# Graph layer with routed experts on one core: one normalized tensor for the router and the experts, and expert outputs weighted in place and added in DRAM

## The reference, cut to what matters

```python
xn = layernorm(x)
x = x + gnn(xn, W, edges) + linear_attention(xn, wq, wk, wv, wo)
#   gnn: h = xn @ W; deg = 1 + in-degree without self edges; dinv = 1/sqrt(deg)
#        out[src] = sum over edges and loops of dinv[src] * dinv[dst] * h[dst]
xt = layernorm(x)                                   # normalized once
logits = xt @ Wr + br                               # 8 experts
top_p, top_idx = top_k(softmax(logits), 2); weights = top_p / top_p.sum()
xn2 = layernorm(xt)                                 # normalized twice
xe = xn2[None] * ln_g[:, None] + ln_b[:, None]      # per expert
h = gelu(xe @ W1 + b1)
y = h @ W2 + b2
out = x + (weights[:, :, None] * y[top_idx]).sum(axis=1)
```

## Time and profile before

| | us |
|---|---|
| median of 3 runs | 2603.84 |
| the profiled execution, device time | 2604.59 |
| its span, first to last instruction | 2602.70 |
| edge sums, 450 to 1589.5 | 1139.5 |
| routing, 1589.5 to 1680 | 90.5 |
| picks up to the first expert product, 1680 to 1771.2 | 91.2 |
| experts, 1771.2 to 2536.9 | 765.7 |
| output, 2536.9 to 2602.7 | 65.8 |

### The profile page before, as it was taken

How to read it: one execution, slowest core, us unless ns; L and a number is a source line. 1 busy time by engine, 2 the same in 40 slices (tenths; PEclk the granted TensorE clock), 3 DMA queues, 4 the chain that set the end, 5 groups by cost and what they waited for, 6 DMA issues and landing times.

```text
span 2602.7 us, 56074 instructions
## 1 busy us (share of the span) xinstructions
PE 2180.6 (84%) x12041; PEld 1796.9 (69%) x12042; DVE 1328.7 (51%) x2437; ACT 1200.7 (46%) x3274; POOL 1324.0 (51%) x1388
## 2 busy tenths in 40 slices
PE   0999994888888888888888866658999999999990
PEld 0677773666666666666666645517999999999980
DVE  8799996565666666666666546651111111111116
ACT  2444441666666666666666644502333333333320
POOL 6766565677777777777777761002222222222220
PEclk9999997899999999999999997558999999999995
DMA  4000003333333333333333494434555555555539
GB/s 135 1 1 1 1 1 112 93 105 105 104 104 105 105 105 105 105 105 105 105 104 104 122 80 69 132 124 137 180 180 180 181 179 182 181 180 181 181 108 297
DMA packets 139535, 304.96 MB, mean 117 GB/s; under 512 B 29056, under 2 KB 77101, under 8 KB 139376
## 3 DMA queue, kind: packets, MB, share of 16 engines
q0 software_dynamic: 59232, 143.39, 21.9%
q1 hardware_dynamic: 80272, 161.23, 17.4%
HBM read 270.55 MB, written 33.98 MB: 117 GB/s over the span
## 4 chain that ended last, share of the span: by engine, by line
PE 57%; DMA 20%; DVE 9%; issue 5%; DVEq 4%; POOL 3%; ACT 0%; SPq 0%; ACTq 0%; POOLq 0%
PE B L1403 18%; DMA BIG<-table,W2A 18%; PE B L1499 15%; PE B L1508 14%; DVEq L665 3%; DVE BIG L660 3%; PE B L1392 2%; PE B L1465 1%; POOL BIG L507 1%; PE B L1309 1%; PE B L1342 1%; DVE W1A L1061 1%; POOL W2A L483 1%; PE B L1487 1%; PE B L1326 1%
## 5 line engine op out<-in xcount | busy, mean ns | idle before, releaser
L507 POOL DMA_INDIRECT BIG<-table,W2A x880 | 834.5, 948 | 301.3 <-issue 202.4
L547 DVE TENSOR_TENSOR ACC<-ACC,B 128x512 f32 x880 | 605.4, 688 | 451.9 <-PE B L1403 312.3
L1403 PE MATMUL B<-BIG 128*128 128x256 f32 x1760 | 429.8, 388 | 83.9 <-DMA BIG<-table,W2A 81.7
L1403 PE MATMUL B<-BIG,W2A 128*128 128x256 f32 x1760 | 427.6, 386 | 85.9 <-DMA BIG<-table,W2A 85.8
L1079 ACT ACTIVATE BIG<-B,SMALL 128x128 f32<-128x128 f32 (+1 forms) x889 | 251.1, 387 | 506.3 <-PE B L1499 506.3
L1403 PEld LDWEIGHTS B<-BIG 128*128 128x128 f32 x1760 | 322.4, 191 | 182.9 <-issue 143.6
L1403 PEld LDWEIGHTS B<-BIG,W2A 128*128 128x128 f32 x1760 | 316.8, 190 | 174.3 <-issue 137.2
L1499 PEld LDWEIGHTS B<-BIG,W1A 128*128 128x128 f32 x3360 | 393.6, 193 | 7.9 <-DVE BIG L550 2.6
L1499 PE MATMUL B<-BIG,W1A 128*128 128x128 f32 x3360 | 394.4, 276 | 2.0 <-DVE BIG L550 2.0
L1508 PE MATMUL B<-W2A,BIG 128*128 x1680 | 380.1, 379 | 0.7 <-DVE ACC L547 0.7
L1508 PEld LDWEIGHTS B<-W2A,BIG 128*128 128x128 f32 x1680 | 311.0, 190 | 39.1 <-issue 1.1
(11 more groups left out here) (208 smaller groups left out, 2203.8 us busy)
## 6 DMA issues: line engine op xcount, KB each, us to landing
W1A<-in_w SPq DMA_DIRECT2D x105, 1024.0 KB, 5.1
BIG<-table,W2A POOLq DMA_INDIRECT x880, 2.8
W2A<-in_w SPq DMA_DIRECT2D x1, 8192.0 KB, 30.1
table<-ACC SPq DMA_DIRECT2D x7, 896.0 KB, 7.1
token_x<-BIG SPq DMA_DIRECT2D x49, 128.0 KB, 1.7
W2A<-in_x SPq DMA_DIRECT2D x1, 6144.0 KB
W1A<-pick_y SPq DMA_DIRECT2D x4, 896.0 KB, 10.8
W2A<-pick_y SPq DMA_DIRECT2D x4, 896.0 KB, 11.2
```

Of the source, the lines that this page charges most:

```text
L507: pool.indirect_dma_start(G[h][:, u, :], None, table, bass.IndirectOffsetOnAxis(ap=idx_s[h][:, u:u + 1], axis=0)).then_inc(gath[h][u // 2] ...
L547: return dve.tensor_tensor(o, a, b, op)
L1403: last = mm(B[u][:, k * D:(k + 1) * D], OH[h % 2][:, u, k * P:(k + 1) * P], G[h][:, u, :], start=True, stop=True)
```

## The change

In the edge sums, `acc` now takes the input and the attention too, each multiplied by `sdeg` = sqrt(deg), so that `acc * dinv` is the new x without a separate `residual` pass: `add_attention` writes to `acc`, and a new `add_inputs` does one VectorE instruction for each of 49 tiles.

In routing, one normalized tensor remains, `xs2`. Its scales come from the statistics of `acc` (with `dinv` worked in), it is both stored to `token_x` and transposed for the router, in pairs of tiles, and the logits are multiplied by `unscale` afterwards, which turns the twice normalized rows back into once normalized ones for the router. Groups are 6, 10, 16 and 17 tiles. All copies of transposes are ScalarE's, 512 columns at a time. Behind them ScalarE multiplies `acc` by `dinv` in place (49 instructions), and then signals `res_ready`.

In the picks, `pc_tile` and `pc_tokens` get a second buffer, and ScalarE makes the second half of `pc_tokens`.

In the experts, the two gates of every node are transposed on TensorE, stored to a table `gates` in DRAM, and gathered by slot (`gather_gate`, 128 numbers for each tile). `sums` in DRAM starts as a copy of `acc` (6.5 MB, one SP transfer). `outputs` adds `b2` into `y_plain`, which frees the bank, and multiplies by the gate into `y_out`; the scatter adds its rows to `sums` in DRAM instead of writing `pick_y`, and each scatter waits until the one before has landed, since the two picks of a node may be in neighbouring tiles. ScalarE's index copies are gone.

The output is one DRAM to DRAM transfer from `sums` to `out`.

```diff
 sync:
-            with sp.Fori(0, NT // RG) as g:
-                store_group(g)
-            sp.wait_ge(x_done, 1)
+            for j in range(NPAIR):
+                n = min(2, NT - 2 * j)
+                sp.wait_ge(xs_ready, 2 * j + n)
+                sp.dma_start(token_x[2 * j * P:(2 * j + n) * P, :]..., xs2[j % 4][:, 0:n, :]).then_inc(xs_out[j % 4], 16)
             sp.dma_start(W2A[:, :]..., w2...).then_inc(w2_in, 16)
...
             for t in range(4):
                 load_w1(t, t)
+            sp.wait_ge(gates_T_ready, 1)
+            sp.dma_start(gates[0:PICKS * P, :]..., gates_T...).then_inc(gates_out, 16)
+            sp.wait_ge(res_ready, 1)
+            sp.dma_start(sums.rearrange("(t p) d -> p t d", p=P), acc).then_inc(sums_set, 16)
             with sp.Fori(1, ST // 4) as i:
...
-            (loads of pick_y in 9 parts, stores of out in 9 parts)
+            sp.dma_start(out.rearrange("(p a) d -> p (a d)", p=125), sums[0:N_NODES, :].rearrange("(p a) d -> p (a d)", p=125)
+                         ).then_inc(o_sent, 16)
 gpsimd:
+            def scatter_y(t):
+                pool.wait_ge(y_ready, t + 1)
+                if t >= 1:
+                    pool.wait_ge(y_sent[(t - 1) % 2], 16 * ((t + 1) // 2))
+                pool.indirect_dma_start(sums, bass.IndirectOffsetOnAxis(ap=slot_row[:, t:t + 1], axis=0),
+                                        y_out[t % 2], None, compute_op=ALU.add).then_inc(y_sent[t % 2], 16)
...
+            pool.wait_ge(sums_set, 16)
+            for t in range(ST):
+                scatter_y(t)
+                if t + 3 < ST:
+                    gather_gate(t + 3)
+                if t + 5 < ST:
+                    gather_x(t + 5)
 vector:
+            ch.add(dve.tensor_copy(sdeg, col[12][:, 0:NT]))
+            ch.add(tt(dinv2, dinv, dinv, ALU.mult))
...
             def add_attention(t):
+                dve.drain()
-                tt(xt, xt, B[7][:, 0:D], ALU.add).then_inc(q_added, 1)
+                dve.scalar_tensor_tensor(out=a, in0=B[7][:, 0:D], scalar=sdeg[:, bass.ds(t, 1)], in1=a,
+                                         op0=ALU.mult, op1=ALU.add).then_inc(q_added, 1)
+            def add_inputs(t):
+                dve.drain()
+                dve.scalar_tensor_tensor(out=a, in0=xt, scalar=sdeg[:, bass.ds(t, 1)], in1=a, op0=ALU.mult, op1=ALU.add)
...
             def slot_digits(g, s):
+                when(dve, tk_v, pc_used, g - 1)
                 tt(pc_at[s], pc_digits, cols(slot_at, P), ALU.is_equal)
-                tt(pc_tile, ...); dve.drain(); when(dve, tk_v, pc_used, g)
-                tt(pc_tokens[:, 0:ST, :], ...); ts(pc_tokens[:, ST:2 * ST, :], pc_tile, row_1, ALU.mult)
+                tt(pc_tile[s], ...); dve.drain(); dve.sem_inc(pc_ready, 1)
+                tt(pc_tokens[s][:, 0:ST, :], ...); dve.drain(); dve.sem_inc(pc_ready, 1)
...
             def outputs(t, s):
-                when(dve, tk_v, y_sent[s], (t - s) * 8)
-                tt(y_out[s], B[7][:, 0:D], b2_all[:, bass.ds(e * D, D)], ALU.add).then_inc(y_ready, 1)
+                tt(y_plain, B[7][:, 0:D], b2_all[:, bass.ds(e * D, D)], ALU.add).then_inc(y_free, 1)
+                dve.drain()
+                when(dve, tk_v, gate_in[s], (t - s) * 4 + 16)
+                when(dve, tk_v, y_sent[s % 2], (t - s % 2) * 8)
+                ts(y_out[s % 2], y_plain, slot_gate[:, bass.ds(t, 1)], ALU.mult).then_inc(y_ready, 1)
+                dve.drain()
 scalar:
+                    cp(xs2[j % 4][:, t % 2, :], acc[:, t, :], ACT.Identity, scale=rstd2[:, t:t + 1], bias=nmr2[:, t:t + 1]
+                       ).then_inc(xs_ready, 1)
+                    if t % 2 == 1 and t >= 3:
+                        transposed_x2(t // 2 - 1)
...
+            for t in range(NT):
+                last = cp(acc[:, t, :], acc[:, t, :], scale=dinv[:, t:t + 1])
+            last.then_inc(res_ready, 1)
...
+                cp(pc_tokens[g % 2][:, ST:2 * ST, :], pc_tile[g % 2], scale=row_1).then_inc(pc_rows, 1)
 tensor:
-                when(pe, tk_t, y_ready, t)
+                when(pe, tk_t, y_free, t)
```

More of the change, by code:

```diff
@@ L66 @@
 SLOTS = ST * P
[L67 to L70, removed]
+LGROUPS = [range(a, b) for a, b in zip((0, 6, 16, 32), (6, 16, 32, NT))]
+NPAIR = (NT + 1) // 2
 PICKS = TOPK * NT
@@ L79 @@
 assert NGR <= 32 and UNROLL * 5 < 24
-assert NT % RG == 0 and STEPS >= NT + 2 + 2 * E // BATCHES and min(RLAG) >= 3
+assert all(g.stop % 2 == 0 for g in LGROUPS[:-1])
 assert PICKS % PC == 0 and PC % 2 == 0 and (PICKS // PC) % 2 == 1 and ST % 4 == 1
@@ L178, in gps_layer @@
         col = [small(k, 50) for k in range(10, 24)]
-        rstd2a, rstd2, nmr2 = (small(k) for k in range(24, 27))
+        sdeg, dinv2, var2 = small(7), small(8), small(0)
+        stat_in, stat_root = grid(SMALL, 1000, 2, 50), grid(SMALL, 1100, 2, 50)
+        unscale, rstd2, nmr2 = small(1), small(25), small(26)
         q_all = grid(W1A, 0, KD, NT * P)
@@ L242, in gps_layer @@
         NE = NT * E
[L243 to L246, removed]
+        R0 = KD * H * 4 + E * D
+        logits, pick0, pick1, both, tmp, rank, totals, runs = (grid(W1A, R0 + NE * k, NT, E) for k in range(8))
+        xs2 = [grid(BIG, 512 * s, 2, D) for s in range(4)]
+        x2T = [grid(BIG, 2048 + 512 * s, 2 * KD, P) for s in range(4)]
         wr_s, br_s = grid(BIG, 5448, KD, E), piece(BIG, 5464, E)
@@ L417, in _ @@
             sp.wait_ge(y_sent[1], 16 * (ST // 2))
[L419 to L435, removed]
+            sp.dma_start(out.rearrange("(p a) d -> p (a d)", p=125), sums[0:N_NODES, :].rearrange("(p a) d -> p (a d)", p=125)
+                         ).then_inc(o_sent, 16)
+            sp.wait_ge(o_sent, 16)
         @block.gpsimd
@@ new lines, in _ @@
+            pool.wait_ge(slots_ready, 1)
+            for t in range(4):
+                gather_x(t)
+            pool.wait_ge(rows_known, 1)
+            pool.wait_ge(gates_out, 32)
+            for t in range(3):
+                gather_gate(t)
+            gather_x(4)
+            pool.wait_ge(sums_set, 16)
[5 more added lines that the diff above has]
+                    gather_x(t + 5)
@@ L798, in add_step @@
                 add_sums(i * BATCHES + 2)
+                if not isinstance(i, int) or i < NT:
+                    add_inputs(i)
                 add_sums(i * BATCHES + 3)
@@ L887, in _ @@
-            residuals(0, range(RG))
-            dve.drain()
-            statistics(0, range(RG))
-            dve.drain()
-            norms(0)
-            group(0)
-            with dve.Fori(1, NT // RG - 1) as g:
-                group(g)
-            dve.sem_inc(x_done, 1)
-            group(NT // RG - 1, True)
+                dve.sem_inc(norm2_ready, 1)
+            statistics(LGROUPS[0])
+            variances(LGROUPS[0])
+            for k, g in enumerate(LGROUPS):
+                if k + 1 < len(LGROUPS):
+                    statistics(LGROUPS[k + 1])
+                scales(k, g)
+                if k + 1 < len(LGROUPS):
+                    variances(LGROUPS[k + 1])
@@ L1518, in step @@
                 second_product(t, s % 2)
+            pe.wait_ge(gates_T_ready, 1)
             inputs(0, 0)
```

370 lines of the change are left out of this document (154 added, 216 removed).

## The result

The changed kernel took 2581.02 us (median of 4 runs, 2579.07 to 2583.70) beside 2603.84 us for the kernel before (median of 3 runs): a ratio of 0.9912, 95% interval 0.9895 to 0.9930. A fourth run of the kernel before took 10714.63 us and is left out. The change is faster by 23 us, under 1%, where 69 us were forecast, and the time ends 1 us outside the range. The profiled execution took 2579.8 us (span 2577.9).

A forecast was written before the change was run, and what follows sets the result against it. Bounds: GpSimd in the edge sums, TensorE in the experts, the order of waits elsewhere. Terms +3.5 - 20.5 - 1.8 - 10.2 - 1.7 + 0 + 0 - 38.3 = -69.0 gave 2535 us; range 2500 to 2580.

The forecast's parts named there:

- Edge sums: Edge-sum stage: VectorE hides the added instructions and drains, GpSimd's issue is held up slightly; +3.5 us.
- the prediction's own sign of being wrong: Wrong if edge sums end more than 10 us later, steps exceed 7.3 us, or the copy takes over 40.
- GpSimd's issue beside `add_inputs`: Edge sums: each `add_inputs` may delay a gather's issue by 0 to 0.41 us; 3.2 us taken, up to 20 possible.
- Routing: Routing, to the reading of the logits: the bound passes from ScalarE and the norms to TensorE; -20.5 us.
- Logits to picks: Between logits and picks: the wait for `slot_experts` shrinks as `w2`'s load starts earlier; -1.8 us, bounds 0 and -2.84.
- picks: Picks: second buffers let VectorE and ScalarE work beside TensorE, removing six gaps of 1.87 us; -10.2 us.
- first product: From picks to first expert product: fewer VectorE instructions before the signal, GpSimd reads the index itself; -1.7 us.
- Sums' store: Store of `sums` before the experts: 20.5 us plus latency, hidden with 4 us of reserve; 0, or +25 if 52 us.
- loop: Experts' loop: unchanged at 7.29 us a tile while the scatter's landing and issue stay below that; 0.
- output: From the last tile's result to the end: 65.8 us becomes 27.5, with a 23.0 us copy; -38.3 us.
- the rival of the slow scatter: Experts: adding scatters slow the loop; a landing of about 7.6 us makes the kernel slower than before; chance 0.08.
- The clock: Rival: TensorE's clock rises in routing, picks or both; 2519 us with one, 2502 with both; chance 0.13.

The follow-up runs named there:

- e1: The changed kernel without the 49 `add_inputs` instructions, input rows left out of the result: 2528.48 us, 0.9721 of the kernel before.
- e5: The changed kernel with VectorE waiting once for two sums of a batch instead of once for each, full result: 2531.25 us, 0.9723 of the kernel before.
- e6: The changed kernel with `add_inputs` reading and writing the input rows, without its drain, input rows left out of the result: 2543.77 us, 0.9773 of the kernel before.
- e8: The kernel before with VectorE waiting once for two sums instead of once for each: 2603.02 us, 1.0000 of the kernel before.
- e7: The changed kernel with scatters that write instead of add, sums and first expert left out of the result: 2579.54 us, 0.9907 of the kernel before.

## Why the prediction was wrong

- **Edge sums: the step that failed.** "... the reader sees 303.7 us idle for 40 steps, 7.6 us a step, so VectorE hides them, and the two drains." The idle time of the earlier trace rows was not free time: some 230 of the 303.7 us (639 x 0.36) are what the queue takes for each add. The true reserve was 0.6 us a step. The added 1.77 us lifted the step 1.26 us above GpSimd's pace, 60.5 us over 48 steps, of which the lead of the gathers took up 11. Measured +49.5 for +3.5; the prediction's own sign of being wrong, edge sums that end more than 10 us later, came. e1, e5, e6 and e8 show it. The row to read was the distance from start to start of neighbouring adds, not the group's idle sum.
- **The price that I did name, GpSimd's issue beside `add_inputs`, does not exist here.** Gathers take 948 ns in both kernels. Each of the 49 `add_inputs` (L760) runs beside a gather, and each of these takes 0.94 or 0.95 us (one at 1013.76). By the Trainium skill's page "SBUF — State Buffer", section "Who interferes with whom", a VectorE instruction with two SBUF inputs contends with a GpSimd instruction that reads SBUF; taken for the issue of a gather, this trace does not agree. The same section says that a `tensor_tensor` was not seen to stall DMAs, which fits these gathers. The earlier trace rows were of another pair, a far longer VectorE instruction beside scatters.
- **Routing** was right in mechanism: TensorE sets the pace at the lower clock. Two tiles take 2.45 us (1697.63 to 1700.08), not 2.34; -18.75 for -20.5. The terms written there add up to about 1658.7, not 1659.5.
- **Logits to picks, picks, first product:** -16.7 for -13.7. Groups follow one another without gaps, and `slot_experts` is no longer waited for, the bound named in the text. The picks' own terms give -10.4 (6 x 1.87 - 0.6 - 0.2), not -10.2.
- **Sums' store, loop, output:** the store took 22.7 us. GpSimd's first scatter waited 14.5 us for it, and nothing of that shows in the sum; the copy took 21.9 for 23.0. The adding scatter's landing was mis-sized: 3.0 taken, 6.4 us measured (median, single ones up to 8.3 between 1800 and 1900 us), with an issue of 1.63 for 0.98 us. The last six scatters, behind the last load of `w1` and the last gathers of rows, land in 3.7 to 3.8 us; with 6.5 before, the traffic beside them is the likely cause, which no run separates. GpSimd waited 2.8 us for it in each tile (289.1/102) and started a scatter some 1.5 us behind VectorE's result (1845.05 to 1846.57) instead of 0.3 as for the last tiles; TensorE kept its step. But less than 1 us lay between this landing and a step of 7.25: the rival of the slow scatter was closer than its chance of 0.08 said. How much longer a landing the loop would bear, no run shows.
- **The clock did not rise** in routing (0.52) or in the picks (0.50), though their gaps went.

The range failed with the one term: its bounds, 0 to +20, were bounds of one mechanism and not of the step. The time lies only 1 us outside because the range was widened for other mishaps, not because this step was bounded.

## What to carry to other kernels

Before calling an engine idle, take the distance from start to start of its neighbouring instructions in a loop: where it is constant whatever the releaser, the queue itself takes that time, and neither the busy share nor the idle sum tells the room left. Price an added instruction by what it lengthens that distance, with its drain, waits and register work; at this batch's end the drain was four fifths of it. Then set the sum against the pace of the engine that leads now, and ask how much lead its buffers give.

## What the runs showed of the hardware

- A wait against a register with its counter step costs 0.18 us of VectorE's queue: adds stand 1.05 us apart with it and 0.87 without, in e5 and in the changed kernel's unrolled step alike, where the wait is against a fixed number and steps no counter:

```profile
1510.57 0.69 DVE L542 TENSOR_TENSOR ACC<-ACC,B 128x512 f32 x1 [0.86 <-PE B L1350]
1511.44 0.69 DVE L542 TENSOR_TENSOR ACC<-ACC,B 128x512 f32 x1 [0.19 <-issue]
```

- A drain ahead of a 0.48 us instruction cost 0.8 us at a batch's end.
- An indirect DMA of 128 KB that adds in DRAM took GpSimd 1.63 us to issue instead of 0.98 for a plain one (e7). It landed in 6.4 us beside the loads of `w1` and the gathers, and in 3.7 to 3.8 behind the last of them; the plain one of e7 in 2.4.
- A DRAM to DRAM transfer of 6.40 MB took 21.9 us; 8.39 MB from DRAM into the chip's memory took 30.1: 292 and 279 GB/s, nearly the same, though the first both reads and writes DRAM.
